# Seven maxima blocks of 128 query rows, and a rearranged end of the attention part, in a cross-attention and mixture-of-experts kernel

## The chip, the cores and the metric

The kernel runs on one core of a Trainium2 chip. The metric is the device time of one execution in microseconds (us). Engines are named as in the profile: PE (TensorE, matrix products; PEld is its loading of stationary operands), DVE (VectorE), ACT (ScalarE), POOL (GpSimd), and SP (SyncE), which here only issues transfers.

## The reference

The input x is 16 sequences of 224 rows of 512 numbers, and each has a context of 750 rows of 384. All is float32.

```
x = x + cross_attention(layernorm(x), ctx)       # 16 heads of 32, each with its softmax over 750 keys, then Wo
y = layernorm(x)
logits = cos(y, centroids) + y @ w_route.T       # 8 experts
gates  = softmax over the two largest logits, 0 elsewhere
x = x + sum over e of gates[e] * (gelu(y @ w1[e] + b1[e]) @ w2[e] + b2[e])
```

Only the two chosen experts of a row have a gate that isn't 0, so 2 x 3584 pairs of row and expert are enough.

## The kernel before

**Attention.** The work is cut into 64 groups (a sequence has four groups of four heads each). A Python loop over g from -2 to 68 writes out the order on each engine by hand; `first`, `second`, `third` and `fourth` are its bodies for g % 4 = 0 to 3, one of each on every engine, and `after(g)` follows each. It is a software pipeline. In turn g, PE projects Q and K of group g+2, finds maxima for group g+1, makes the scores and the weighted values of group g, and the denominators of group g-1. Products of float32 operands are made as three products of a high and a low part (`split3`). The high part is rounded by ACT, the low part is what DVE or POOL subtracts.

**Maxima.** The softmax needs a number to subtract for each query. `score_for_max(g, u)` multiplies one block of queries (stationary) by all 750 keys (moving, in two products of 376 columns), high parts only, into PSUM tile X, and DVE's `maximum(g, u)` reduces X to one column of `mx`. There are XU = 8 blocks of 112 rows for the 4 x 224 queries of a group. X is one tile, so block u+1 waits for DVE's reduction of block u. `transpose_max` turns `mx`, ACT negates it into `mneg`, and `put_max` (SP) copies it into a row of the stacked queries `qst`, from which the scores get their subtraction.

**Softmax sums.** ACT's `exps(g, s)` makes the probabilities from scores, 12 pieces for a group. POOL's `add_step(g, 0..4)` adds the six tiles of 125 keys in five steps into `psum_p`, `denominators(g)` on PE sums over the partitions with a matrix of ones, DVE's `invert` and `normalise` divide the output by it, ACT's `o_hi` and DVE's `o_lo` split it for the output projection (`project_o`).

**Second layernorm.** Per sequence b: DVE's `residual` and `y_stats`, POOL's `y_rsqrt` (16 small steps, two roots; semaphore newton2), ACT's `y_apply`, PE's transposes, ACT's copies to y_T, PE's `logits`, DVE's `keep_logits`.

**Weights of the experts.** w1 and w2 come in 16 pieces of 128x1024 (0 to 7 are w1). SP loads them (`load_pieces`), ACT rounds the high part (`w_part` on ACT), DVE subtracts the low part (`w_part` on DVE), in the turns 62 to 66 and one piece at the end.

**Routing.** After the loop DVE picks the two experts of each row (semaphore route), PE counts with a triangular matrix of ones, DVE makes the place of each pair in a list sorted by expert (place), and a table of which row stands in which of the 63 tiles of 128 slots is made on PE by one-hot products: `find_columns`, then `find_rows` in four chunks per choice, two choices. `table_done` ends it.

**Experts.** POOL gathers 128 rows with an indirect DMA, PE transposes (`fold_x`), multiplies by w1 (`up`), ACT does gelu, PE transposes (`fold_h`) and multiplies by w2 (`down`), DVE adds b2, ACT multiplies by the gate, and POOL adds the rows to the output with an indirect DMA.

What sets the order is the written-out sequence on each engine: an engine does its instructions strictly one after the other, and waits for semaphores in between. Names touched: `score_for_max` and `maximum` (L1540, L1072), `transpose_max` (L1549), `y_rsqrt` (from L539), `add_step` (L488, L491), `constants` (from L586), `w_part` (L846 on ACT, L1149 on DVE), `after` on each engine, `denominators` (L1590), `find_columns` (L1340, L1344), `find_rows` (L1352), `project_o` (L320 to L322 into M), `up` (L1804 to L1808), `down` (L1825 to L1827).

## Time and profile before

| | us |
|---|---|
| median of 3 runs | 1652.7 (1652.04 to 1652.82) |
| the profiled execution | 1648.43 |
| its span, first to last instruction | 1646.6 |
| PE busy in the span | 1524.2 (93%) |
| POOL, DVE, ACT busy | 1080.2, 1030.6, 944.2 |
| mean granted clock of PE | 0.964 |

```profile
PE   4899999999999999999999999999999743899997
PEclk9999999999999999999999999999999765899999
```

Each digit is a slice of 41 us, in tenths. PE is busy nearly throughout, except in the slices from the 32nd on (1276 us), where attention has ended and the experts haven't begun. PEclk is the granted clock: 1.2 GHz at 0.5 and 2.4 GHz at 1. The profiled execution is one run, shorter than the median of the timed ones by 4.3 us.

### The profile page before, as it was taken

How to read it: one execution, taken by the hardware profiler on the slowest of the kernel's cores; microseconds unless marked ns; L12 is line 12 of the kernel's file. 1: busy time of each engine (PE TensorE's matmuls, PEld its weight loads, DVE VectorE, ACT ScalarE, POOL GpSimd, SP SyncE). 2: the span in 40 equal slices, each digit the busy share in tenths (PEclk: the TensorE clock that was granted, in tenths of full speed). 3: DMA queues.
4: the chain of work that ended last, by engine and by line, in shares of the span. 5: the costliest groups of instructions: out<-in, count | busy, mean ns of one | idle time of the engine just before them, and what ended most of it. 6: DMA issues, size and time to landing. Idle time of an engine off the chain costs nothing.

```text
span 1646.6 us, 33344 instructions
## 1 busy us (share of the span) xinstructions
PE 1524.2 (93%) x11534; PEld 1247.4 (76%) x11534; DVE 1030.6 (63%) x1475; ACT 944.2 (57%) x2055; POOL 1080.2 (66%) x931
## 2 busy tenths in 40 slices
PE   4899999999999999999999999999999743899997
PEld 4777777778787878787877877877777433798996
DVE  5556666666666676766666666666665568344443
ACT  4456666666666666666666666665665440455554
POOL 3366767676767677776676777777775740477675
PEclk9999999999999999999999999999999765899999
DMA  7556666666667676767666757676756733578785
GB/s 193 97 81 111 101 134 123 110 124 108 127 110 134 111 129 112 131 110 139 112 130 107 136 101 144 101 140 101 140 91 120 187 122 35 136 135 147 135 148 90
DMA packets 113394, 199.29 MB, mean 121 GB/s; under 512 B 20448, under 2 KB 49280, under 8 KB 113104
## 3 DMA queue, kind: packets, MB, share of 16 engines
q1 hardware_dynamic: 98992, 165.81, 54.4%
q0 software_dynamic: 14240, 31.35, 10.5%
q8 instruction: 98, 1.61, 0.5%
q14 instruction: 64, 0.52, 0.1%
HBM read 64.29 MB, written 38.66 MB: 63 GB/s over the span
## 4 chain that ended last, share of the span: by engine, by line
PE 86%; DVE 5%; ACT 3%; POOL 2%; issue 1%; DMA 1%; POOLq 0%; DVEq 0%; SPq 0%; ACTq 0%
PE M L320 12%; PE S L1563 12%; PE M L321 12%; PE M L322 12%; PE X L1540 11%; PE O L1579 10%; ACT pr L781 2%; PE M L1825 2%; PE X L1807 2%; PE X L1808 2%; PE X L1806 2%; PE M L1826 2%; PE M L1827 2%; PE M L1590 2%; PE S L1796 2%
## 5 line engine op out<-in xcount | busy, mean ns | idle before, releaser
L1072 DVE TENSOR_REDUCE mx<-X 112x1 f32<-112x752 f32 x512 | 480.6, 939 | 356.0 <-PE X L1540 353.9
L491 POOL TENSOR_TENSOR psum_p<-psum_p,pr 125x896 f32<-125x896 f32 x256 | 543.9, 2124 | 172.6 <-ACT pr L781 149.1
L781 ACT ACTIVATE pr<-S 125x448 f32<-125x448 f32 x768 | 395.0, 544 | 224.4 <-PE S L1563 216.6
L1563 PEld LDWEIGHTS S<-qst,kst 128*125 128x125 f32 x1536 | 234.7, 189 | 113.0 <-ACT pr L781 51.2
L1563 PE MATMUL S<-qst,kst 128*125 128x224 f32 x1536 | 287.3, 291 | 27.1 <-ACT pr L781 21.2
L1540 PE MATMUL X<-kh_s,q_own 128*112 128x376 f32 x1024 | 272.0, 347 | 8.4 <-DVE mx L1072 7.9
L1540 PEld LDWEIGHTS X<-kh_s,q_own 128*112 128x112 f32 x1024 | 153.9, 176 | 48.0 <-issue 26.8
L1579 PE MATMUL O<-pr,v 125*32 125x224 f32 x3072 | 188.6, 364 | 1.7 <-ACT pr L781 1.7
L488 POOL TENSOR_TENSOR psum_p<-pr 125x896 f32<-125x896 f32 x64 | 135.6, 2119 | 80.1 <-ACT pr L781 79.9
L475 POOL TENSOR_TENSOR ctx_l<-ctx_r,ctx_h 128x750 fp32r<-128x750 f32 x48 | 85.4, 1811 | 74.7 <-ACT ctx_h L696 74.7
L320 PE MATMUL M<-ctx_h,wk_h 128*128 128x376 f32 (+1 forms) x384 | 130.0, 339 | 0.0
L321 PE MATMUL M<-ctx_l,wk_h 128*128 128x376 f32 (+1 forms) x384 | 129.4, 337 | 0.0
L322 PE MATMUL M<-ctx_h,wk_l 128*128 128x376 f32 (+1 forms) x384 | 128.8, 335 | 0.0
L1579 PEld LDWEIGHTS O<-pr,v 125*32 125x32 f32 x3072 | 81.3, 110 | 62.3 <-issue 23.1
L662 POOL DMA_INDIRECT out<-y_out,table_t x63 | 99.9, 1586 | 41.4 <-ACT y_out L1003 23.3
L654 POOL DMA_INDIRECT xg<-rows_d,table_x x63 | 62.4, 990 | 86.3 <-DVE settled L1400 43.0
L320 PE MATMUL M<-wv_h,ctx_h 128*125 128x512 f32 x288 | 116.8, 405 | 0.0
L322 PE MATMUL M<-wv_h,ctx_l 128*125 128x512 f32 x288 | 113.6, 394 | 0.0
L321 PE MATMUL M<-wv_l,ctx_h 128*125 128x512 f32 x288 | 113.5, 394 | 0.0
L1079 DVE RECIPROCAL M<-M 128x224 f32<-128x224 f32 x64 | 99.8, 1559 | 21.7 <-PE M L1590 21.6
L738 ACT ACTIVATE q_own<-qh_s,own 128x224 fp32r<-128x224 f32 x256 | 102.6, 472 | 2.1
L1062 DVE SCALAR_TENSOR_TENSOR kl_s<-M,bk_s,kh_s 128x376 fp32r<-128x376 f32 (+1 forms) x128 | 77.0, 602 | 14.3 <-ACT kh_s L749 14.1
(222 smaller groups left out, 3005.1 us busy)
## 6 DMA issues: line engine op xcount, KB each, us to landing
kst<-kh_s SPq DMA_DIRECT2D x128, 375.0 KB, 7.3
kst<-kl_s SPq DMA_DIRECT2D x64, 375.0 KB, 10.4
ctx_r<-ctxT SPq DMA_DIRECT2D x48, 375.0 KB, 12.2
qst<-qh_s SPq DMA_DIRECT2D x128, 112.0 KB, 2.8
rows_d<-x_res SPq DMA_DIRECT2D x32, 448.0 KB, 10.6
w_l<-w SPq DMA_DIRECT2D x16, 512.0 KB, 7.0
x_ln<-x SPq DMA_DIRECT2D x17, 448.0 KB, 11.0
qst<-ql_s SPq DMA_DIRECT2D x64, 112.0 KB, 3.0
```

Of the source, the lines that this page charges most:

```text
L320: pe.matmul(out, lhs[0], rhs[0], start=first, stop=False)
L321: pe.matmul(out, lhs[0], rhs[1], start=False, stop=False)
L322: return pe.matmul(out, lhs[1], rhs[0], start=False, stop=last)
L488: pool.tensor_tensor(out=total, in0=tiles[0], in1=tiles[1], op=ALU.add).then_inc(sum_step, 1)
L491: pool.tensor_tensor(out=total, in0=total, in1=tiles[half], op=ALU.add).then_inc(sum_step, 1)
L662: pool.indirect_dma_start(out=out[:, :], out_offset=bass.IndirectOffsetOnAxis(ap=table_t[:, i:i + 1], axis=0), in_=y_out[:, i % YO, :], in ...
L738: act.activation(q_own[:, g % 2, j, :], qh_s[:, g % 2, :], ACT.Copy, scale=own[:, j:j + 1]).then_inc(own_done, 1)
L781: act.activation(pr[0:KP, (3 * g + p) % 2, j, :, :], S[0:KP, n % SB, 0:2 * NQ].rearrange("p (i n) -> p i n", i=2), ACT.Exp).then_inc(exp_d ...
L1072: dve.tensor_reduce(mx[0:QP, u:u + 1], X[0:QP, :, 0:HALF[0][1]], AX.XY, ALU.max).then_inc(max_done, 1)
L1540: last = pe.matmul(X[0:QP, i, 0:w], q_own[:, g % 2, j, QP * qt:QP * (qt + 1)], kh_s[:, g % 2, off:off + w], start=True, stop=True)
L1563: last = pe.matmul(S[0:KP, n % SB, NQ * h:NQ * (h + 1)], kst[:, i, j, o:o + KP], qst[:, i, j, :], start=True, stop=True)
L1579: last = pe.matmul(O[HD * j:HD * (j + 1), 0:NQ], v[0:KP, 2 * p + i, HD * j:HD * (j + 1)], pr[0:KP, (3 * g + p) % 2, j, i, :], start=(p == ...
```

## The change

- Maxima: XU is 7. A block is 128 consecutive queries out of the group's 896, head by head, so a block can hold queries of two heads. Everything that had 112 rows here has 128. `maximum(g + 1, 7)` and `score_for_max(g + 1, 7)` are gone from all four bodies.
- Last roots: for the last two sequences (b = 14 and 15, LATE = 14) `y_rsqrt` is left out on POOL, and DVE does `late_root(b)` at the end of `y_stats(b)`, with 27 steps of Newton's method. `roots` and `shifted` count the semaphore.
- Sums: for the last group POOL leaves out steps 3 and 4, and `denominators` adds the last two tiles on PE, as two more sets of four products.
- Weight parts: ACT does 11 of them after turn 64 and 5 after turn 67; DVE 6 after turn 64, 4 after 66 and 6 behind `table_done`. PE waits for w1's before `up(0)` and for all before the first `down`. The first three loads on SP stand behind `put_max(63)`.
- `constants` on POOL moves from turn 63 to after turn 64. b2 (2 MB in SBUF) is loaded at the end of SP's loop, once the last output projection is done, instead of behind `table_done`; memory is laid out again for that, and `hot_row` becomes a ring of three chunks.
- `keep_clock(n)` on PE issues n products of 128x128 by 512 columns into a PSUM bank that nobody reads: 6 after turn 64, 22 after turn 65, 22 after the loop, 42 behind the counts, 10 ahead of each of the two choices' one-hot products, and 26 ahead of the first tile.

```diff
-XU = 8
+XU = GH * NQ // P
+LN_STEPS, Y_STEPS, LATE_STEPS = 8, 16, 2 * RSQRT_STEPS + 3
+LATE = B - 2
+ACT_EARLY = E + 3
+ROWS = 3 * CHUNK
...
+        def roots(b):
+            return Y_STEPS * min(b, LATE) + LATE_STEPS * max(0, b - LATE)
...
@@ on SP
-                    if g == GROUPS - 2:
-                        wait_full(sp, "K1", GROUPS - 1)
-                        load_pieces(0, 3)
...
-                        load_pieces(3, E)
+                        load_pieces(0, E)
+                wait_full(sp, "O1", B - 1)
+                sp.dma_start(b2_all[:, :, :], b2.rearrange("(a e) n -> a e n", a=1).broadcast_to([P, E, D])
+                             ).then_inc(b2_in, 16)
                 sp.wait_ge(route, 15)
...
-                sp.wait_ge(table_done, 1)
-                sp.dma_start(b2_all[:, :, :], b2.rearrange("(a e) n -> a e n", a=1).broadcast_to([P, E, D])
-                             ).then_inc(b2_in, 16)
...
@@ on POOL
-                    if not 0 <= g < GROUPS:
+                    if not 0 <= g < GROUPS or (g == GROUPS - 1 and i >= 3):
...
@@ on ACT
-                    if g == GROUPS - 2:
-                        for n in range(3):
-                            w_part(n)
...
-                        for n in range(3, E):
-                            w_part(n)
...
+                        wait_full(act, "den", GROUPS - 1)
+                        act.wait_ge(b1_both, 32)
+                        for n in range(ACT_EARLY):
+                            w_part(n)
+                    if g == GROUPS + NG - 1:
+                        for n in range(ACT_EARLY, W_PIECES):
                             w_part(n)
...
@@ on DVE
-                    dve.tensor_reduce(mx[0:QP, u:u + 1], X[0:QP, :, 0:HALF[0][1]], AX.XY, ALU.max).then_inc(max_done, 1)
+                    dve.tensor_reduce(mx[:, u:u + 1], X[:, :, 0:HALF[0][1]], AX.XY, ALU.max).then_inc(max_done, 1)
+                def late_root(b):
+                    n, m = roots(b), mv2[0:QP, :, :]
+                    v, y, tmp, off = ve2[0:QP, :], rstd2[0:QP, :], rtmp2[0:QP, :], shift2[0:QP, :]
+                    sq, ln = square[0:QP, :], length[0:QP, :]
+                    dve.wait_ge(y_var, QT * (b + 1))
+                    dve.wait_ge(yn_done, QT * b)
+                    rsqrt(dve, newton2, n, m[:, :, 1], EPS, ALU.add, v, y, tmp)
+                    n += RSQRT_STEPS
+                    dve.scalar_tensor_tensor(out=off, in0=m[:, :, 0], scalar=-1.0, in1=y, op0=ALU.mult,
+                                             op1=ALU.mult).then_inc(newton2, 1)
+                    wait_free(dve, "lg1", b - 1)
+                    dve.tensor_tensor(out=sq, in0=m[:, :, 1], in1=y, op=ALU.mult).then_inc(newton2, 1)
...
+                    rsqrt(dve, newton2, n + 3, sq, NORM_EPS2, ALU.max, v, ln, tmp)
...
+                    if b >= LATE:
+                        late_root(b)
...
                     if g == GROUPS:
-                        for n in range(E, E + 3):
+                        for n in range(6):
                             w_part(n)
...
-                        dve.wait_ge(newton2, Y_STEPS * B)
-                        for n in range(E + 3, 2 * E - 1):
+                        for n in range(6, 10):
                             w_part(n)
...
-                w_part(2 * E - 1)
...
                 dve.tensor_copy(settled[:, :], ones[:, 0:1]).then_inc(table_done, 1)
+                for n in range(10, W_PIECES):
+                    w_part(n)
...
@@ on PE
-                        last = pe.matmul(X[0:QP, i, 0:w], q_own[:, g % 2, j, QP * qt:QP * (qt + 1)],
+                        last = pe.matmul(X[:, i, 0:w], own_q[:, P * u:P * (u + 1)],
                                          kh_s[:, g % 2, off:off + w], start=True, stop=True)
...
+                    parts = [psum_p[0:KP, g % 2, :, :]]
+                    if g == GROUPS - 1:
+                        pe.wait_ge(sum_step, 5 * g + 3)
+                        pe.wait_ge(exp_done, 12 * (g + 1))
+                        parts += [pr[0:KP, (3 * g + 2) % 2, :, h, :] for h in range(2)]
...
+                def keep_clock(n, ready=w1_h[:, 0, 0:2, :].rearrange("p c n -> p (c n)")):
+                    for _ in range(n):
+                        pe.matmul(HP[:, 1, :], ready[:, 0:P], ready, start=True, stop=True)
+
                 def after(g):
+                    if g == GROUPS:
+                        keep_clock(6, wo_h[:, 0, :])
+                    if g == GROUPS + 1:
+                        pe.wait_ge(ew_hi, 1)
+                        keep_clock(22)
...
-                    score_for_max(g + 1, 7)
...
+                keep_clock(22)
                 pe.wait_ge(masks, 1)
                 pe.wait_ge(route, 12)
...
+                keep_clock(42)
                 for i in range(2):
+                    keep_clock(10)
                     pe.wait_ge(col_done, 2 * (i + 1))
...
+                keep_clock(26)
                 pe.wait_ge(which_done, 1)
                 pe.wait_ge(table_done, 1)
                 pe.wait_ge(b1_both, 32)
-                pe.wait_ge(ew_lo, W_PIECES)
                 fold_x(0)
                 fold_x(1)
+                pe.wait_ge(ew_lo, E)
                 e = expert_of(0)
                 up(0, e)
                 fold_h(0)
+                pe.wait_ge(ew_lo, W_PIECES)
```

## Rows read from the trace of the kernel before

**Rows 1.** Busy us by engine in three stretches, PE's granted clock, DMA share, GB/s.

```profile
97.40:1285.00 1187.60, 1166.23 (x9226) 937.39 (x9225) 784.27 (x1095) 734.05 (x1651) 837.33 (x712) 1.00 0.66 118
87.20:90.60 3.40, 3.40 (x23) 1.99 (x22) 1.16 (x2) 2.80 (x5) 2.39 (x2) 0.53 0.00 0
1346.70:1411.50 64.80, 26.98 (x120) 25.00 (x121) 44.24 (x75) 6.36 (x11) 11.07 (x22) 0.50 0.34 73
```

**Rows 2.** Groups by line, 400 to 1200: busy us, mean ns, idle before.

```profile
L320 PEld LDWEIGHTS M<-ctx_h,wk_h 128*128 128x128 f32 x240 | 45.3, 189 | 0.0
```

**Rows 3.** Timeline of PE, turns 37 and 39: start, us, instructions, idle before.

```profile
804.34 0.50 PE L1540 MATMUL X<-kh_s,q_own 128*112 128x376 f32 x2
804.68 0.39 PE L320 MATMUL M<-wo_h,oT_h 128*112 128x512 f32 x1
...
844.82 0.48 PE L1563 MATMUL S<-qst,kst 128*125 128x224 f32 x2 [0.83 <-ACT pr L781]
```

**Rows 4.** Timeline of PE in turn -1.

```profile
48.74 0.60 PE L1540 MATMUL X<-kh_s,q_own 128*112 128x376 f32 x2 [1.03 <-DVE mx L1072]
50.47 0.34 PE L1549 MATMUL M<-id_s,mx 112*8 112x112 f32 x1 [1.12 <-DVE mx L1072]
```

**Rows 5.** Timelines of DVE and POOL: a step at the start, two instructions at 837.

```profile
19.22 0.15 DVE L45 TENSOR_TENSOR ctmp<-cinv 8x1 f32<-8x1 f32 x1
...
837.41 2.13 POOL L488 TENSOR_TENSOR psum_p<-pr 125x896 f32<-125x896 f32 x1
...
837.47 2.32 DVE L1093 SCALAR_TENSOR_TENSOR oT_l<-o_s,bv_s,oT_h 128x224 fp32r<-128x224 f32 x1
```

**Rows 6.** Timeline of POOL before turn 63.

```profile
1297.07 10.41 POOL L491 TENSOR_TENSOR psum_p<-psum_p,pr 125x896 f32<-125x896 f32 x4 [3.97 <-ACT pr L781]
```

**Rows 7.** Timeline of DVE between attention and experts.

```profile
1308.65 1.57 DVE L1079 RECIPROCAL M<-M 128x224 f32<-128x224 f32 x1
...
1321.51 10.33 DVE L1149 TENSOR_TENSOR w_l<-w_l,w_h 128x1024 fp32r<-128x1024 f32 x5 [0.67 <-ACT w_h L846]
1331.76 1.55 DVE L1079 RECIPROCAL M<-M 128x224 f32<-128x224 f32 x1
...
1350.45 4.63 DVE L1149 TENSOR_TENSOR w_l<-w_l,w_h 128x1024 fp32r<-128x1024 f32 x4 [5.17 <-POOL length L570]
...
1355.88 0.42 DVE L1259 TENSOR_REDUCE most<-lgs 112x32 f32<-112x256 f32 x1
...
1394.87 0.15 DVE L1400 COPY settled<-ones 128x1 f32<-128x1 f32 x1
```

**Rows 8.** Timeline of ACT in the same stretch.

```profile
1318.06 2.31 ACT L781 ACTIVATE pr<-S 125x448 f32<-125x448 f32 x4
...
1334.16 4.83 ACT L846 ACTIVATE w_h<-w_l 128x1024 fp32r<-128x1024 f32 x5
1347.82 1.52 ACT L812 ACTIVATE x_res<-x_ln,shift,rstd 112x512 f32<-112x512 f32 x2 [8.82 <-POOL shift L552]
```

**Rows 9.** Timeline of PE in the same stretch, and the first tile.

```profile
1328.63 0.98 PE L1590 MATMUL M<-psum_p,ones 125*32 125x224 f32 x8 [6.48 <-POOL psum_p L491]
...
1385.48 7.01 PE L1786 MATMUL M<-hot_tok,hot_row 112*128 112x64 f32 x32 [2.06 <-DVE hot_row L1352]
...
1406.04 0.58 PE L1804 MATMUL X<-b_hl,ones_r 128*128 x1 [0.78 <-DVE xTs L1404]
...
1412.69 0.40 PE L1825 MATMUL M<-w_h,hTs 128*128 x1
```

**Rows 10.** The chain that ended last, in order of time: start, us, what.

```profile
1334.88 0.74 PE M L320
...
1336.05 0.43 PE M L322
...
1339.84 0.23 PE M L322
```

**Rows 11.** The gathers into xg: time to landing.

```profile
DMA to landing us min/median/max: 3.3/4.3/7.3
```

More of the change, by code:

```diff
@@ L171, in expert_phase @@
         rw = sb("rw", [P, DC, 2 * E])
-        mneg = sb("mneg", [XU, QP], F32R)
-        zone_end = here[0]
+        mneg = sb("mneg", [XU, P], F32R)
+        here[0] = zone_end = max(here[0], zone_c + 4 * (E * D + ROWS * P + TT * LC))
         bq_s, bk_s, bv_s = sb("bq_s", [P, NG]), sb("bk_s", [P, NG]), sb("bv_s", [P, NG])
@@ L316, in residual_of, with shifted @@
             return x_ln if b == B - 1 else x_res
+        def roots(b):
+            return Y_STEPS * min(b, LATE) + LATE_STEPS * max(0, b - LATE)
+        def shifted(b):
+            return roots(b) + (LN_STEPS if b < LATE else RSQRT_STEPS + 1)
         def split3(pe, out, lhs, rhs, first, last):
@@ L531, in y_rsqrt @@
                 def y_rsqrt(b):
-                    if not 0 <= b < B:
+                    if not 0 <= b < LATE:
                         return
@@ L599, in after @@
                         return
+                    constants()
                     pool.wait_ge(pv_done, 3 * GROUPS)
@@ L639, in fourth @@
                     y_rsqrt(b - 1)
-                    constants(g)
                     add_step(g, 0)
@@ L1151, in after @@
                 def after(g):
-                    if g == GROUPS - 2:
-                        for n in range(3):
-                            w_part(n)
                     if g == GROUPS - 1:
@@ L1158, in after @@
                                           op=ALU.subtract).then_inc(b1_lo, 1)
-                        for n in range(3, E):
-                            w_part(n)
                     if g == GROUPS:
-                        for n in range(E, E + 3):
+                        for n in range(6):
                             w_part(n)
@@ L1548, in transpose_max @@
                     pe.wait_ge(max_done, XU * (g + 1))
-                    pe.transpose(out[0:XU, 0:QP], mx[0:QP, :], id_s[0:QP, 0:QP]).then_inc(full, 1)
+                    pe.transpose(out[0:XU, 0:P], mx[:, :], id_s[:, :]).then_inc(full, 1)
                 def score(g, s):
@@ L1587, in denominators @@
                     out, full = claim("den", g)
-                    pe.wait_ge(sum_step, 5 * (g + 1))
-                    for j in range(GH):
-                        last = pe.matmul(out[HD * j:HD * (j + 1), 0:NQ], ones[0:KP, :], psum_p[0:KP, g % 2, j, :],
-                                         start=True, stop=True)
+                    parts = [psum_p[0:KP, g % 2, :, :]]
[3 more added lines that the diff above has]
+                        parts += [pr[0:KP, (3 * g + 2) % 2, :, h, :] for h in range(2)]
+                    else:
+                        pe.wait_ge(sum_step, 5 * (g + 1))
+                    for n, part in enumerate(parts):
+                        for j in range(GH):
+                            last = pe.matmul(out[HD * j:HD * (j + 1), 0:NQ], ones[0:KP, :], part[:, j, :],
+                                             start=n == 0, stop=n == len(parts) - 1)
                     last.then_inc(full, 1)
@@ L1694, in second @@
                     score(g, 9)
-                    score_for_max(g + 1, 7)
                     project_o(b - 1, 1, 1)
@@ L1728, in third @@
                     score(g, 9)
-                    score_for_max(g + 1, 7)
                     values(g, 1)
@@ L1765, in fourth @@
                     transpose_y(b - 1, 1)
-                    score_for_max(g + 1, 7)
                     score(g, 10)
```

76 lines of the change are left out of this document (39 added, 37 removed).

## The prediction

> **What bounds the kernel now.** I read the windows first, then the groups by line of the steady middle, then the timelines of PE and of the engines that PE waits for. From 97 to 1285 us PE is busy 1166 of 1188 us, at full granted clock; DVE (784), ACT (734) and POOL (837) have a third of that time free [rows 1]. There a microsecond that leaves PE's queue leaves the run, unless something else ends last at that place. From 1285 to 1411 us it is another kernel: a chain in which DVE, POOL, ACT and PE wait for each other, with PE busy 27 of its last 65 us and at half clock [rows 1]. There PE's instructions are cheap and everything on the chain counts. From 1412 us the 63 expert tiles fill PE again; the change leaves them alone.
>
> **Maxima: seven blocks for eight.** Per head group score_for_max issues two products of 376 moving columns per block, over 64 groups: 1024 products become 896. The queries become the stationary operand's columns, 128 instead of 112. A load of 128 columns takes 189 ns where K does it [rows 2], beside the products, since PEld overlaps PE; the K products, with the same 376 moving columns, follow each other no slower than the maxima's. So I price a new pair like an old one: from the start of the eighth block to the start of what follows is 804.68 - 804.34 = 0.34 us [rows 3]. (If a product's cost went with the stationary columns, 7x128 = 8x112, the gain would be 0; that is the other end.) DVE loses one tensor_reduce in eight, off the path.
> Where the block only fills a wait, it gains nothing. In every fourth group it stands between the y transposes and score 10; score 10 waits 0.83 us for the exponentials behind it, which ACT does after copying y_T out of PSUM [rows 3]. Those copies start from the transposes, which stand before the block, so the wait grows by 0.34 and the group gains 0. That is 14 of the groups up to 61. In the other three kinds output projection, logits or values follow, all longer than an exponential.
> At the start the block costs more, since PE waits for DVE between blocks: 50.47 - 48.74 = 1.7 us in group -1 [rows 4]; with about 0.7 and 1.4 in groups 0 and 1, where the same two waits are shorter, 3.7 us. Groups 2 to 61: 46 x 0.34 = 15.8. **Main part: -19.5 us.**
>
> **Last roots on DVE.** The 27 tiny instructions of late_root are queued on DVE before invert(62). Alone, such a step takes 0.15 us [rows 5] and some 0.04 to the next (0.19, 5.1 us in all, the same as POOL's chain of 5.2). But they don't run alone: at 837.47 a DVE instruction with two SBUF inputs, usually 0.44 us, took 2.32, until POOL's addition that began at 837.41 had ended [rows 5]. 21 of the 27 have two SBUF inputs. late_root(14) would start at 1299.9, and POOL adds four times from 1297.07 on [rows 6], now 2.13 us each since no weight parts slow it, to 1305.7. So DVE gets through its three first steps and about one per addition; at 1305.8, 21 are left. Ten fit in until add_step(63, 0), from 1307.8 to 1309.9, blocks it again; the rest is done at 1311.9. invert(62), at 1308.65 before [rows 7], then starts 3.2 us later, and with it o_hi(62), the exponentials 4 to 7 of the last group that ACT has behind it, the values, y_apply and the transposes. Exponentials 8 to 11, which ran from 1318.06 to 1320.4 [rows 8], end at 1323.6. Bounds: 0 (free slots between additions; -2.7, since additions end earlier) and +6.
> The Trainium skill, page SBUF — State Buffer (the single rule on ports), says the same: a DVE instruction with two SBUF inputs waits for a GpSimd instruction that reads SBUF, for its whole length. It also says that DVE's one-input instructions can contend in a two-port mode; that would add the six tensor_scalar steps, at most 1 us more here.
>
> **Sums partly on PE, and weight parts later.** Three of ACT's weight parts stood ahead of the last group's first exponential. Without them (3 x 0.97 us at most [rows 8]) scores 0 to 2 go earlier, but score 3 stands behind den(62), which waits for POOL's additions to 1305.8: worth nothing. SP issues the loads of these three behind the maxima's transfer instead of ahead of it; POOL makes its constants after group 64's work, idle since 1320.9, in time for the b1 transfers. Before, invert(63) started at 1331.76 because DVE sat in five weight parts, 10.33 us at 2.07 each beside POOL's four additions [rows 7]. After: the exponentials end at 1323.6. den's four products took 0.98 us at half clock [rows 9], so the last eight of the values take 1.7 and den's twelve now 2.9 (PE sums the last two tiles itself, so nothing waits for POOL): 1328.3. invert, normalise, o_hi and o_lo take 3 us: 1331.3. PE has been dense since 1323.7 (values, den, logits 14, six dummies) and should be at full clock by now, so logits and dummies end about there, and output projection starts at 1332 instead of 1334.88 and takes 24 x 0.23 = 5.6 [rows 10]: 1337.6.
> Now DVE is late: after(64) puts six weight parts ahead of the residual. They cost 1.15 each without POOL (4.63 / 4 [rows 7]): 1332.0 + 6.9 = 1338.9; ACT's halves take 0.97 [rows 8] and keep ahead. Statistics start at 1340.2, 3.3 earlier than before. late_root(15) meets an idle POOL: 13 steps to the shift, 2.5 us, against 2.8 on POOL; y_apply at 1344.4, before 1347.82 [rows 8]. The 22 dummies behind the projection (5.1 us at full clock) end at 1342.7, before the transposes at 1346. DVE: late_root ends 1347.0, mask, four weight parts, 1351.9; logits 15 are ready by 1350. The routing (DVE most) starts at 1352.8, before 1355.88 [rows 7]: **-3.1**. This is a small part of what the moved work seems to free.
> Routing to table: the same DVE chain of 39 us, less the weight part in it (1.15) and about 0.35 for the two count products, of 512 columns each, at full clock: **-1.5**. The ring of three row chunks stalls nothing: PE takes 1.75 us for a chunk at half clock (7.01 / 4 [rows 9]), DVE makes one in 1.14 and has 4.6 us of columns between the halves.
> Table to first product: up(0) started 11.0 us after the table (1395.02) [rows 7, 9]. Its first fold waited for a gather that landed in 7.3 us, the longest of all, beside the 2 MB load of b2; the median is 4.3 [rows 11]. With b2 moved forward (issued about 1344 behind the stores of x and x_n; the gates' small transfers queue behind its 2 MB, but aren't needed before 1391) the first lands at about +5.2. But six weight parts now stand before x_low(0): 6.9 + 0.7 + 0.1 = 7.7: **-3.3**. Bounds: -5 (no weight parts in the way) and +2 (each also waits about 1 us for a gather's POOL instruction). I take the undisturbed one, as the four parts beside POOL's DMA issue at 1350.45 took 1.16. The page named above would side with it: descriptors need the write side, these parts only the shared read side.
>
> **Dummies.** 138 products of 512 columns: 32 us at full clock (0.23 each), 59 at half (0.43) [rows 10]. What they give: from up(0) to down(0) took 1412.69 - 1406.04 = 6.65 us at half clock [rows 9]; at full 13 x 0.12 for up, then gelu, fold, up again: 4.25. Idle ahead of the first fold is about 3.4 us, so I expect the clock to hold mostly: **-2.1**. Where the cover goes: 52 stand between the count products and the first row chunk, 14.2 us apart; at full clock they take 12.1, if the first 16 run at half 15.2, which delays PE but not DVE; all at half 22.4, 8 too many. The 26 before the gather have 8.7 us.
>
> **Sum.** -19.5 - 3.1 - 1.5 - 3.3 - 2.1 = -29.5 us. The profiled execution took 1648.4 (span 1646.6), so 1618.9 by it; the runs' median is 1652.7, 4.3 above, and 29.5 off that is **1623.2**. Half of the tail's possible gain is handed back by late_root(14) and by weight parts ahead of the residual.
>
> **Rivals.**
> A, late_root isn't blocked as I price it, and slots between additions are enough: the tail gains 3 to 6 more, 1618. For it: additions are separate instructions with gaps; against it: the one row where a DVE instruction paid the whole addition. 0.2.
> B, dummies in the way: the clock stays at half for most of the tail, as for the 65 us before 1411.5 [rows 1]. They then overrun by about 1 (behind projection), 3 (behind logits), 8 (52) and 3 (26), and the 2.1 and 0.35 don't come: +15 with what the ring adds, 1638. Against it: the projection alone, 24 products, was enough for full clock. 0.12.
> C, the block isn't worth 0.34 us: the stream behind it is bound by ACT's exponentials and not by PE in other groups too (third kind: scores 7 to 9 already go at ACT's pace). With half the gain, +9: 1632. Against it: PE idles only 22 us in 1188. 0.12.
> D, the other side of zero: the clock in the main part. A wait of ACT of 2.3 us ahead of 87.2 was followed by a stretch of 3.4 us at half clock, and again at 94 [rows 1], worth 1.7 us each of full work. The wait in each fourth group grows from 0.83 to 1.2. If that drops the clock for two stretches each time, 14 x 3.4 = 48 us is lost against 29.5 won: 1671. It decides from nine such double stretches on. Against it: none of the waits of 0.8 did it. 0.03.
> The changes that don't do what they say at all (products priced by stationary columns) would leave 1643: 0.03.
>
> **How the numbers follow.** My case has 0.5, with its own range 1619 to 1628; A 0.2, B 0.12, C 0.12, D 0.03, the last 0.03. From 1613 (A with its far end) to 1636 (C, and most of B) holds eight in ten. Slower by over 0.2%, which is what a measurement of this kernel can tell from no change: only D, 0.03, and some of B and C together: 0.04. Within 0.2%: 0.02. Faster: 0.94.
>
> **What would show it.** The step between max transposes of the steady groups: three of four shorter by 0.34 us, the fourth unchanged, with its wait at about 1.2. DVE's steps in late_root(14): some of 2 us, invert(62) later than add (62, 4) by 6 us. den(63) right behind the values; DVE's weight parts ahead of the residual. The first gather landing in 4 to 5 us, DVE in weight parts as x_low(0) becomes ready. Full clock from the projection to the tiles. The forecast is wrong if PE's idle time in the main part grows by more than 10 us, or if dummies end later than what stands behind them was ready.

## The result

| | before | changed |
|---|---|---|
| median of the timed runs | 1652.37 (4 runs, 1651.11 to 1652.82) | 1635.62 (4 runs, 1632.63 to 1635.79) |
| the profiled execution, its span | 1648.43, 1646.6 | 1635.56, 1633.7 |
| mean granted clock of PE | 0.964 | 0.984 |

The ratio is 0.9897, 95% interval 0.9881 to 0.9912: 16.7 us faster, where 29.5 were forecast. The time lies in the range (1613 to 1636), at its slow end, 12.4 us above the predicted 1623.2. The changed kernel was measured once more in a later session, after_again below: there it is 22.6 us faster than before, so 7 to 13 us of the forecast gain are missing.

Where the 12.9 us between the two profiled executions come from. The end of turn 60, the last quiet place before the tail, is taken from the third-last max transpose; the rows behind it count from there.

| | before | changed | difference | forecast |
|---|---|---|---|---|
| end of turn 5 | 172.42 | 165.68 | -6.7 | |
| end of turn 60 | 1261.30 | 1253.49 | -7.8 | -19.5 |
| to the table's end | 133.3 | 129.2 | -4.1 | -4.6 |
| table to the third tile's h low part | 24.0 | 18.9 | -5.1 | -5.4 |
| from there to the end of the span | 227.9 | 232.1 | +4.1 | 0 |

So nearly the whole miss lies in the main part: 11.7 us, and 0.8 in the two rows of the tail. The last row is probably no part of it. The first three gains add up to 17.0 us, which is what the medians show (16.7), while the profiled execution of before is 3.9 us shorter than its own median; the last section has what is known of that.

The chain that ended last, as shares of the span, from the pages; first before, then changed:

```profile
PE 86%; DVE 5%; ACT 3%; POOL 2%; issue 1%; DMA 1%; POOLq 0%; DVEq 0%; SPq 0%; ACTq 0%
```

```profile
PE 62%; POOL 18%; issue 9%; DVE 6%; ACT 4%; DMA 1%; POOLq 0%; DVEq 0%; SPq 0%; ACTq 0%
POOL psum_p L509 12%; PE M L342 8%; PE S L1581 8%; PE M L343 8%; PE M L344 8%; PE X L1558 7%; PE O L1597 6%; POOL ctx_l L493 3%; ACT pr L797 2%; PE X L1840 2%; PE X L1842 2%; PE X L1841 2%; POOL x_res L525 2%; PE M L1615 2%; PE M L1859 2%
```

The engine that was said to have a third of its time free now carries a fifth of the chain. The time between max transposes tells in which bodies (mean of 13 or 14 turns each, 6 to 60; the runs' names are those of the experiments):

| us per turn | before | changed | maxima_only | bo_later | both | ctx_split | guard |
|---|---|---|---|---|---|---|---|
| `first` | 19.92 | 19.63 | 19.62 | 19.62 | 19.62 | 19.63 | 19.63 |
| `second` | 20.69 | 20.90 | 20.67 | 20.44 | 26.30 | 21.42 | 20.42 |
| `third` | 18.68 | 18.70 | 18.70 | 18.70 | 18.44 | 18.43 | 18.44 |
| `fourth` | 19.96 | 19.97 | 19.96 | 19.96 | 19.96 | 19.97 | 19.97 |

`first` pays back 0.29, `fourth` nothing, as forecast. `second` and `third` were to give 0.34 each, gave nothing, and `second` grew by 0.21. Over the turns 6 to 60 that is 7 us short in `second` and 5 in `third`. Groups by line from 400 to 1200 us (count, busy us, mean ns, idle before and what ended it), POOL's addition of bo and PE's denominators; before, then changed:

```profile
L507 POOL TENSOR_TENSOR x_res<-x_res,bo_s 112x512 f32<-112x512 f32 x20 | 25.4, 1291 | 18.8 <-DMA x_res<-x 18.8
L1590 PE MATMUL M<-psum_p,ones 125*32 125x224 f32 x324 | 23.6, 362 | 0.0
```

```profile
L525 POOL TENSOR_TENSOR x_res<-x_res,bo_s 112x512 f32<-112x512 f32 x20 | 25.2, 1283 | 33.8 <-DMA x_res<-x 33.8
L1615 PE MATMUL M<-psum_p,ones 125*32 125x224 f32 x320 | 23.4, 363 | 6.4 <-POOL psum_p L509 6.3
```

And one `second` (turn 41, in which POOL waited longest) and the `third` behind it in the changed kernel's timelines of POOL and PE (start, us):

```profile
860.80 2.53 POOL L525 TENSOR_TENSOR x_res<-x_res,bo_s 112x512 f32<-112x512 f32 x2 [4.27 <-DMA x_res<-x]
863.28 4.36 POOL L509 TENSOR_TENSOR psum_p<-psum_p,pr 125x896 f32<-125x896 f32 x2
...
867.79 0.59 PE L1615 MATMUL M<-psum_p,ones 125*32 125x224 f32 x8 [1.27 <-POOL psum_p L509]
...
873.92 5.33 POOL L493 TENSOR_TENSOR ctx_l<-ctx_r,ctx_h 128x750 fp32r<-128x750 f32 x3 [4.21 <-ACT ctx_h L712]
879.22 8.89 POOL L509 TENSOR_TENSOR psum_p<-psum_p,pr 125x896 f32<-125x896 f32 x4
...
888.25 0.59 PE L1615 MATMUL M<-psum_p,ones 125*32 125x224 f32 x8 [0.20 <-POOL psum_p L509]
```

In `second`, POOL stood 4.27 us in `add_bo`, for a load, and the two additions behind it ended 1.27 us too late for den. In `third`, den waited for a chain that begins with ACT's ctx_high behind exponential 7: 5.33 of ctx_low, then four additions, end to end.

How near the two chains were to den before the change can be read from the traces (medians over 13 or 14 turns each; the load's times count from the start of `second`, the last two rows give the time from the end of POOL's last addition to the start of den):

| us | before | maxima_only | changed | bo_later | guard |
|---|---|---|---|---|---|
| `second`: x_res load issued | -1.88 | -0.59 | -0.58 | -0.53 | -1.21 |
| `second`: load landed | 1.91 | 3.25 | 3.54 | 3.34 | 2.32 |
| `second`: last addition to den | 1.32 | 0.15 | 0.15 | 4.87 | 4.85 |
| `third`: last addition to den | 0.15 | 0.15 | 0.15 | 0.15 | 1.88 |

Where den waits for the addition, 0.15 us pass between the two. `third` shows that same 0.15 before the change: there was next to no slack. `second` had some 1.2 us in the median turn, more than the 0.34 of a block, and lost it another way: SP issues the load when the stores of x_n have landed, these took 11.8 us instead of 11.0 in a turn that had become shorter, and the load landed 1.6 us later in the turn.

### The profile page after: what moved, and what is told of

Its sections match the earlier page's. It is cut to its first block, busy times and chain, and to the rows that moved or that the text cites. A ratio compares the mean times of both kernels' runs of the same rounds, so it can differ in the third digit from the quotient of the medians.

```text
span 1633.7 us, 33542 instructions
## 1 busy us (share of the span) xinstructions
PE 1534.6 (94%) x11560; PEld 1251.7 (77%) x11560; DVE 961.4 (59%) x1465; ACT 943.3 (58%) x2055; POOL 1066.8 (65%) x897
## 4 chain that ended last, share of the span: by engine, by line
PE 62%; POOL 18%; issue 9%; DVE 6%; ACT 4%; DMA 1%; POOLq 0%; DVEq 0%; SPq 0%; ACTq 0%
POOL psum_p L509 12%; PE M L342 8%; PE S L1581 8%; PE M L343 8%; PE M L344 8%; PE X L1558 7%; PE O L1597 6%; POOL ctx_l L493 3%; ACT pr L797 2%; PE X L1840 2%; PE X L1842 2%; PE X L1841 2%; POOL x_res L525 2%; PE M L1615 2%; PE M L1859 2%
## 5 line engine op out<-in xcount | busy, mean ns | idle before, releaser
L509 POOL TENSOR_TENSOR psum_p<-psum_p,pr 125x896 f32<-125x896 f32 x254 | 536.2, 2111 | 177.9 <-ACT pr L797 154.6
L1079 DVE TENSOR_REDUCE mx<-X 128x1 f32<-128x752 f32 x448 | 421.4, 941 | 366.8 <-PE X L1558 364.6
L1558 PE MATMUL X<-kh_s,q_own 128*128 128x376 f32 x896 | 241.4, 351 | 5.9 <-DVE mx L1079 5.9
L1558 PEld LDWEIGHTS X<-kh_s,q_own 128*128 128x128 f32 x896 | 145.7, 190 | 43.9 <-issue 35.7
```

The costliest lines, as they stand in the source:

```text
L509: pool.tensor_tensor(out=total, in0=total, in1=tiles[half], op=ALU.add).then_inc(sum_step, 1)
L1079: dve.tensor_reduce(mx[:, u:u + 1], X[:, :, 0:HALF[0][1]], AX.XY, ALU.max).then_inc(max_done, 1)
L1558: last = pe.matmul(X[:, i, 0:w], own_q[:, P * u:P * (u + 1)], kh_s[:, g % 2, off:off + w], start=True, stop=True)
```

## Experiments

Theory T: a removed block saves PE what was priced, but in `second` a load's wait on POOL (x_res, add_bo, additions, den) and in `third` ctx_high, ctx_low, additions, den end last and take it back. Rivals: R1, a product costs with its stationary columns; R2, the loss comes from something in the rest of the change. All ratios are to the kernel before on the same chip; runs 1 to 4, 5 to 8 and 9 to 12 shared a chip each.

| run | median us | ratio, 95% |
|---|---|---|
| maxima_only | 1636.9 | 0.9945 (0.9930 to 0.9960) |
| rest_only | 1635.2 | 0.9933 (0.9919 to 0.9946) |
| bo_later | 1623.0 | 0.9850 (0.9835 to 0.9864) |
| both | 1701.2 | 1.0330 (1.0313 to 1.0347) |
| ctx_split | 1635.1 | 0.9919 (0.9904 to 0.9934) |
| root14_pool | 1619.2 | 0.9830 (0.9808 to 0.9851) |
| w_split | 1624.8 | 0.9866 (0.9848 to 0.9884) |
| no_dummies | 1627.7 | 0.9882 (0.9865 to 0.9900) |
| after_again | 1629.4 | 0.9862 (0.9846 to 0.9877) |
| guard | 1619.6 | 0.9822 (0.9803 to 0.9842) |
| best | 1619.1 | 0.9802 (0.9788 to 0.9815) |
| few_dummies | 1617.7 | 0.9791 (0.9778 to 0.9804) |

**maxima_only and rest_only**: the change in two halves.

```diff
 # maxima_only: the kernel before, and
-XU = 8
+XU = 7        # with mneg, mx, maximum, score_for_max, transpose_max as in the change
 # rest_only: the changed kernel, with these back at 8 blocks of 112
```

> The kernel before with nothing but the seven maxima blocks; roots, sums, weight parts and dummies as before. My forecast gave this part 19.5 us (3.7 at the start, 46 groups x 0.34). Theory T: PE does save 0.34 per block, but POOL's chains give most of it back: x_res landing later behind the fixed issue of the store of x_n, then POOL's additions, then den in every second kind of group; and ctx_high, ctx_low, additions, den in every third kind. Then the gain is 6 to 8 us, the second kind of group is not shorter than before (20.7 to 20.9 us), and PE's den waits for psum_p by name in many groups. Rival R1 (a product costs with its stationary columns, 7x128 = 8x112): no group is shorter and the gain is the 4 to 5 us of the start. Rival R2 (the main part's loss comes from something in the rest of the change): 17 to 20 us faster than before.

> The changed kernel with eight maxima blocks of 112 queries again; late roots, sums on PE, moved weight parts and dummies stay. My forecast gave these parts 3.1 + 1.5 + 3.3 + 2.1 = 10.0 us. If they act only behind group 61: 9 to 10 us faster than before, and with the maxima alone at 6 to 8 the two gains add up to the whole of 16.7. If the two parts disturb each other (R2), the sum of the two single gains is 5 us or more above 16.7.

Measured by the ratios: -9.1 and -11.0 us, each about 1 more than expected (by the medians -10.5 and -12.2). `second` of maxima_only is 20.67 us, den waited 3.9 us for psum_p, and `first` is 0.30 shorter: T stands; R1 falls, since `first` would not be shorter; R2 falls as the main cause, since the maxima alone fall 7.5 us short of their 19.5 by the end of turn 60 (1249.29). It isn't excluded for the rest: in the changed kernel `second` is another 0.2 us longer and turn 60 ends 4.2 us later than in maxima_only. In no_dummies, whose code up to there is the changed kernel's, turn 60 ends at 1249.89, so part of it is a matter of the execution or the chip. The two gains add up to 20.1 us by the ratios (22.7 by the medians) against 16.7 and 22.6 in the two sessions of the changed kernel: no disturbance between the halves that these intervals can tell.

**bo_later**: the wait for x_res behind the additions' need.

```diff
                 def first(g, b):            # POOL
                     ...
-                    if b < B:
-                        add_bo(b - 1)
                 def second(g, b):
                     add_step(g - 1, 3)
                     add_step(g - 1, 4)
                     add_step(g, 0)
+                    if b < B:
+                        add_bo(b - 1)
                     ctx_low(b + 1)
```

> The changed kernel; POOL's add_bo, which waits for the load of x_res, moves from the end of the first kind of group to behind the first addition of the second kind, so that the additions behind it no longer wait for that load. T: the wait of POOL for x_res goes (about 3 us of it per group of 4), PE's den in the second kind no longer waits, and this kind goes from 20.9 to about 20.35 us; the third kind stays as it is (18.70): 14 groups x 0.5 = 7 us faster than the changed kernel, about 1628.5. R1 or any cause on PE itself: same as the changed kernel within 1 us. If add_bo in the new place makes other additions late instead, 0 to 3 us slower.

`second` fell from 20.90 to 20.44 (expected 20.35), the end of turn 60 came 7.25 us earlier (5.3 against after_again's), and the ratio fell by 0.0047 against the first session (0.0012 against after_again, which the intervals hardly separate; the turns do). POOL no longer waits for the load, den a third as long as before:

```profile
L525 POOL TENSOR_TENSOR x_res<-x_res,bo_s 112x512 f32<-112x512 f32 x20 | 25.5, 1300 | 0.0
L1615 PE MATMUL M<-psum_p,ones 125*32 125x224 f32 x328 | 23.8, 361 | 2.3 <-POOL psum_p L509 2.3
```

**both**: and ctx_high ahead of o_hi, for `third`.

```diff
                 def second(g, b):           # ACT, on top of bo_later
                     xT_part(b + 1, 1)
+                    ctx_high(b + 1)
                     o_hi(g - 1)
                     ...
                     exps(g, 7)
-                    ctx_high(b + 1)
```

> add_bo moved as in the run before, and ACT's ctx_high of the second kind of group moved ahead of its exponentials 5 to 7, so that POOL's ctx_low and the additions behind it start earlier. T: besides the 7 us of the second kind, the third kind of group gets its 0.34 us: 18.70 to about 18.4, 14 x 0.3 = 4 us; in all 10 to 12 us faster than the changed kernel, about 1624.5. If the third kind is held by something else (PE itself, ACT's exponentials), the run is like the one before, or slower by what ctx_high (0.8 us on ACT) delays the exponentials behind it: up to 14 x 0.8 = 11 us.

`third` came out as T says, 18.44. But `second` took 26.30, and the run was 78 us slower than bo_later; I had expected a miss of at most 11, by the exponentials. The timelines of DVE, POOL and PE show it (start, us):

```profile
832.31 5.46 DVE L1100 SCALAR_TENSOR_TENSOR oT_l<-o_s,bv_s,oT_h 128x224 fp32r<-128x224 f32 x1
```

```profile
832.25 5.27 POOL L493 TENSOR_TENSOR ctx_l<-ctx_r,ctx_h 128x750 fp32r<-128x750 f32 x3
...
838.76 0.96 PE L1558 MATMUL X<-kh_s,q_own 128*128 128x376 f32 x2 [3.72 <-DVE mx L1079]
```

DVE's oT_l subtraction of 0.44 us, with two SBUF inputs, began 0.06 us after POOL's and ended only behind three of POOL's, back to back. DVE's next maxima were late, PE stood 3.72 us, and the granted clock was 0.50 for the next 5 us. One collision cost 5.9 us a turn.

**ctx_split**: the same aim, one ctx_high part each behind exponentials 5, 6 and 7.

```diff
                     exps(g, 5)
+                    ctx_high(b + 1, 0)
                     exps(g, 6)
+                    ctx_high(b + 1, 1)
                     exps(g, 7)
-                    ctx_high(b + 1)
+                    ctx_high(b + 1, 2)
```

> add_bo later as in the run bo_later; besides, ACT's three parts of ctx_high in the second kind of group stand one each behind exponentials 5, 6 and 7 instead of all behind 7. The run before, which had all three ahead of exponential 4, made the third kind of group 18.44 us, as T wants, and lost 5.9 us in the second kind, where DVE's oT_l subtraction took 5.46 us beside POOL's three ctx_l subtractions. If that collision is the whole of the loss: here oT_l is through before the first ctx_l, the second kind stays at 20.4 to 20.5, the third goes from 18.70 to 18.45 to 18.6, and the run is 1.5 to 3.5 us faster than bo_later's (0.985 of before), about 0.983. If instead ACT's delayed exponentials were the loss: the second kind grows by 0.3 to 0.8 us, 4 to 11 us slower than bo_later.

oT_l was out of the way and `third` 18.43, but `second` grew by 0.98, for what the second theory named: PE waited for exponentials that stood behind a ctx_high part (0.84 us each). PE's timeline in one turn:

```profile
877.51 0.48 PE L1582 MATMUL S<-qst,kst 128*125 128x224 f32 x2 [0.32 <-ACT pr L796]
878.66 0.96 PE L1598 MATMUL O<-pr,v 125*32 125x224 f32 x16 [0.68 <-ACT pr L796]
```

These 1.00 us are the loss. By the ratios the run is some 11 us slower than bo_later.

**guard**: ctx_high early as in both, at a place where ACT is idle for 2.68 us in ctx_split, waiting for o_s (0.53 us are left of that in guard), and POOL held back by one wait.

```diff
                 def second(g, b):           # POOL, on top of both
                     if b < B:
                         add_bo(b - 1)
+                    if b + 1 < B:
+                        pool.wait_ge(ol_done, g)
                     ctx_low(b + 1)
```

> The kernel of the run both (add_bo later, ctx_high ahead of o_hi, 78 us slower than bo_later), with one wait more: POOL starts its three ctx_low subtractions only when DVE's oT_l subtraction of the same group is through. If the collision of these two is the whole loss: oT_l takes 0.44 us again, the second kind of group goes from 26.3 to 20.3 to 20.5 us, the third stays at 18.44 since ctx_low still ends 2 us earlier than in bo_later and no exponential is held up, and the run is 3 to 5 us faster than bo_later's (0.985): about 0.982 of before. If DVE's maxima or ACT's order were the loss in both: still over 1.0.

POOL waited 0.61 us, oT_l took 0.44, and den no longer waits for POOL at all:

```profile
863.02 0.44 DVE L1102 SCALAR_TENSOR_TENSOR oT_l<-o_s,bv_s,oT_h 128x224 fp32r<-128x224 f32 x1
...
863.54 5.31 POOL L493 TENSOR_TENSOR ctx_l<-ctx_r,ctx_h 128x750 fp32r<-128x750 f32 x3 [0.61 <-DVE oT_l L1102]
...
L1617 PE MATMUL M<-psum_p,ones 125*32 125x224 f32 x328 | 23.8, 362 | 0.0
```

`second` 20.42 and `third` 18.44: the ratio is 0.051 below that of both, some 84 us, for one wait. The end of turn 60 lies at 1241.33, 20.0 us ahead of before, where 19.5 had been forecast for the maxima. The sum agrees partly by luck: 10.9 us of it were won in the turns 6 to 60, where 13.9 had been forecast (41 x 0.34), and 9.1 before them, where some 5 had been. Whether the two moves on POOL would give something to the kernel with eight blocks wasn't tried; its den did not wait.

**root14_pool and best**: the roots of batch 14 back on POOL.

```diff
-LATE = B - 2
+LATE = B - 1      # root14_pool on bo_later; best on guard
```

> add_bo later as in bo_later; besides, LATE is B-1: the roots of batch 14 are POOL's again, only those of batch 15 stay on DVE. My forecast priced late_root(14) on DVE at +3.2 us, since its steps wait for POOL's additions of 2.1 us. If that holds: invert(62) starts within 11 us of the last max transpose as before, the last exponentials end at 21.4 us behind it instead of 25.1, and the run is 3 to 4 us faster than bo_later's. Rival: the den of group 62 waits for POOL, which has 5.2 us of roots ahead of its additions, and gives half of it back: 1 to 2 us. Rival A of my forecast (no blocking): same or slower.

> The kernel of guard, and the roots of batch 14 on POOL again (LATE is B-1). The runs so far: add_bo later -7.5 us against the changed kernel, roots of 14 back on POOL -3.5, guard -3.7. If they add up: 14 to 15 us faster than the changed kernel, ratio to before about 0.980. If the ends of groups 61 and 62 differ between kernels by POOL's order alone, up to 2 us less.

The steps of the tail, counted from the end of turn 60, in one execution each:

| us | before | changed | after_again | rest_only | bo_later | root14_pool | guard | best | no_dummies |
|---|---|---|---|---|---|---|---|---|---|
| invert(62) | 47.4 | 51.3 | 53.4 | 49.2 | 50.5 | 47.6 | 49.8 | 47.7 | 50.5 |
| last exponential ends | 59.1 | 63.5 | 65.6 | 60.9 | 62.4 | 59.2 | 60.8 | 59.4 | 61.6 |
| invert(63) | 70.5 | 67.4 | 69.5 | 64.6 | 66.1 | 61.5 | 63.0 | 61.6 | 63.9 |
| routing starts | 94.6 | 91.5 | 93.6 | 88.7 | 90.2 | 86.7 | 87.1 | 86.6 | 87.9 |
| table done | 133.3 | 129.2 | 131.4 | 126.3 | 127.9 | 124.4 | 125.0 | 124.5 | 125.7 |
| first x_low | 143.9 | 136.4 | 138.5 | 133.5 | 135.0 | 131.5 | 132.1 | 131.6 | 132.8 |
| third h_low | 157.4 | 148.1 | 150.3 | 145.2 | 146.7 | 143.4 | 143.9 | 143.4 | 146.3 |

The changed kernel and after_again are the same code and differ by 2 us in every row, so differences of 1 or 2 us between columns aren't resolved. With the roots on POOL the exponentials end 3.2 us earlier than in bo_later and the table comes 3.5 us earlier: expected 3 to 4. Counted from the last max transpose the exponentials end 6.2 us earlier (18.7 against 24.8), but POOL's roots make turns 61 and 62 3.0 us longer (40.6 against 37.6). In best against guard it is 1.4 and 0.5: there DVE's weight parts, which set the residual, now wait for ACT's high halves (0.85 us). By the times the step isn't resolved: 0.9830 against 0.9850, and 0.9802 against 0.9822, each with intervals that touch.

**w_split**: three of the six weight parts behind the table moved behind x_low(1).

```diff
-                for n in range(10, W_PIECES):
-                    w_part(n)
...
                 dve.wait_ge(which_done, 1)
+                for n in range(10, 13):
+                    w_part(n)
                 x_low(0)
                 e = expert_of(0)
                 x_low(1)
+                for n in range(13, W_PIECES):
+                    w_part(n)
```

> add_bo later as in bo_later; besides, of DVE's six weight parts behind the table three stand ahead of x_low(0) as before and three behind x_low(1). In the changed kernel the table stood 7.69 us ahead of up(0), with DVE in weight parts until x_low(0) was ready. If these set the time: up(0) comes 5.5 to 6 us behind the table, the down product then waits for the last part (3.5 us behind x_low(1)) no longer than for h, and 1.5 to 2 us are won against bo_later. If POOL's gathers, whose issue took 1.9 us each beside these parts, set it: with three parts fewer beside them they take about 1 us again and the gain is the same or up to 1 us more. If the landing of the gather sets it: less than 0.5 us.

No gain. The first x_low came 7.06 us behind the table, in bo_later 7.14: neither theory's 1.5. PE's timeline:

```profile
1377.69 1.07 PE L1653 MATMUL X<-w_h 128*128 128x512 f32 x4
1378.60 0.60 PE L1831 MATMUL S<-id_s,xg 128*128 128x128 f32 x4
...
1385.44 0.92 PE L1831 MATMUL S<-id_s,xg 128*128 128x128 f32 x4 [1.76 <-DVE w_l L1176]
```

The last of the 26 dummies ends where the fold begins, 5.7 us behind the table (the gather had landed 0.8 us before); without dummies the fold began at 5.0 and then took 1.09 us at half clock instead of 0.60. The fold and ACT's rounding of 0.60 us follow before x_low can start, so in bo_later weight parts, dummies and the gather all end last within less than a microsecond. And the expectation that the down product would wait no longer was wrong: the third fold waits 1.76 us for the moved parts, from up(0) to down(0) it takes 8.2 us (4.8 in bo_later), and the third h_low comes 3.5 us later behind the table.

**no_dummies and few_dummies**: without all 138, and without the first 50.

```diff
-                    for _ in range(n):        # no_dummies, on the changed kernel
+                    for _ in range(0):
 # few_dummies, on best: the keep_clock calls 6, 22 and 22 ahead of the counts are gone
```

> The changed kernel as it is (add_bo in its old place), with none of the products that nobody reads. My forecast gave them 2.1 us at up to down of the first tile, and 0.35 for the count products, and let the projection and den get to full clock without them. If that is right: 2 to 5 us slower than the changed kernel (ratio to before 0.991 to 0.993). If they do nothing (the clock falls and rises where real work is): same. If they stood in the way (those behind the logits end as the routing's sums are ready, den and others waited half a us): 1 to 2 us faster.

> The kernel of best without the 50 products that nobody reads in front of the routing (6, 22 and 22); the 88 behind it stay. Without all of them the first tile's up to down took 1.4 us longer, at half clock, and nothing ahead of the table was later, although the last output projection ran at half clock: DVE's weight parts end after it anyway. So the 50 are worth nothing: same as best within 1 us. If they hold the clock for what follows the routing's start: up to 1 us slower. If they stand in the way of the count products: 0.5 us faster.

> The changed kernel once more, on the chip of the runs below, so that they can be held against it. Its two profiled executions are also to tell how far the expert tiles vary: from the third h_low to the end its first profile shows 232.1 us, seven other kernels with the same tiles 226.9 to 228.2. If that is a matter of the execution: 226.9 to 228.2 here, and a ratio of 0.989 to 0.991. If it belongs to the kernel: 232 again.

after_again is a miss on both counts. The ratio is 0.9862, below the expected 0.989 to 0.991, and its interval doesn't meet the first session's; the time from the third h_low to the end is 232.1 us again. So a repetition of the same code moved by 6 us of median (1635.62 and 1629.38, with before at 1652 both times), and what moved it wasn't found.

From the first x_low to the third h_low: 13.5 us without dummies (as before, 13.5), 11.8 in the changed kernel, 12.4 in few_dummies: the dummies save 1.8 us there, forecast 2.1. Up to the table they bring nothing: routing to table takes 37.8 us with and without. The last output projection does start at half clock without them (some nine products, PE's timeline of no_dummies), but DVE's weight parts end only together with it (both at 1324.2):

```profile
1316.87 0.46 PE L342 MATMUL M<-wo_h,oT_h 128*112 128x512 f32 x1 [1.52 <-DVE oT_l L1100]
...
1317.96 0.63 PE L342 MATMUL M<-wo_h,oT_h 128*112 128x512 f32 x1
```

As a whole no_dummies is no slower than the changed kernel (0.9882 against 0.9897 and 0.9862): 1.8 us is below what the times tell. few_dummies is the fastest kernel measured, 0.9791, 11.6 us less than the changed one on the same chip; against best it is the same within the intervals.

## Why the prediction came out as it did

- **Maxima, "46 x 0.34 = 15.8": the step that failed.** The price of a block was near (0.25 to 0.30 in the turns where nothing else ends last). What failed was the condition: "the other three kinds" was argued from PE's next instruction and ACT's exponentials alone, and POOL was dismissed with "a third of that time free" [rows 1]. That is a mean over unlike turns. In `third` before, den already started 0.15 us behind POOL's last addition, as it does where it waits for it: next to no slack, and this, not 30% idle, was the number to look for. In `second` the slack of 1.2 us (0.3 in the tightest turn) was larger than a block in most turns; there the prediction left out that POOL's additions stand behind a load whose time follows the stores and not PE's turns. That wait of 18.8 us in 800 stood in the trace before, and grew to 33.8. Rival C named the size (half the gain lost) but the wrong engine, ACT.
- **The start, 3.7 us**: 4.6 by the end of turn 1. Right in kind (its three terms, 1.7, 0.7 and 1.4, add up to 3.8). The fourth kind with no gain: right, and its wait for the exponentials grew from 0.83 to 1.18 us, as forecast (1.2).
- **late_root(14), +3.2 us**: right. Exponentials 8 to 11 end at 25.1 us behind the last max transpose, 21.4 before: +3.7 (24.7 to 25.2 in after_again, rest_only, bo_later and ctx_split). DVE's timeline in the changed kernel, beside POOL's additions:

```profile
1291.76 0.64 DVE L41 TENSOR_SCALAR ve<-mv 112x2 f32<-112x2 f32 x1
1292.43 0.17 DVE L42 TENSOR_SCALAR rstd<-ve 112x2 int32<-112x2 int32 x1
1292.64 1.99 DVE L43 TENSOR_SCALAR rstd<-rstd 112x2 int32<-112x2 int32 x1
1294.66 0.16 DVE L45 TENSOR_TENSOR rtmp<-rstd 112x2 f32<-112x2 f32 x1
1294.85 2.00 DVE L46 SCALAR_TENSOR_TENSOR rtmp<-rtmp,ve 112x2 f32<-112x2 f32 x1
...
1297.08 1.98 DVE L45 TENSOR_TENSOR rtmp<-rstd 112x2 f32<-112x2 f32 x1
...
1301.54 2.06 DVE L47 SCALAR_TENSOR_TENSOR length<-rtmp,length 112x2 f32<-112x2 f32 x1
...
1304.81 1.57 DVE L1086 RECIPROCAL M<-M 128x224 f32<-128x224 f32 x1
```

```profile
1290.27 8.78 POOL L509 TENSOR_TENSOR psum_p<-psum_p,pr 125x896 f32<-125x896 f32 x4 [5.46 <-ACT pr L797]
1301.51 2.07 POOL L506 TENSOR_TENSOR psum_p<-pr 125x896 f32<-125x896 f32 x1 [2.47 <-ACT pr L797]
```

  One step is lost per addition. Two of the blocked ones (L43, 1.99 us, and in part L41) are tensor_scalar with one SBUF input: what the Trainium skill (SBUF — State Buffer, Who interferes with whom) says, that a tensor_scalar in a two-port mode also waits for GpSimd's whole instruction, fits this; the trace shows that it waited, not the mode.
- **Sums and weight parts, -3.1 to the routing**: measured -3.1 (94.6 to 91.5), but -1.0 in after_again, so that the number agrees so well is luck. The path was the forecast one: projection started 70.5 (before 73.6), DVE's six parts ended behind it and set the residual:

```profile
1324.44 6.89 DVE L1176 TENSOR_TENSOR w_l<-w_l,w_h 128x1024 fp32r<-128x1024 f32 x6
1331.24 1.28 DVE L1109 TENSOR_TENSOR x_ln<-M,x_ln 112x512 f32<-112x512 f32 x2
...
1344.94 0.42 DVE L1276 TENSOR_REDUCE most<-lgs 112x32 f32<-112x256 f32 x1
```

- **Routing to table, -1.5**: 38.7 to 37.8, -0.95. The weight part's 1.15 went; the 0.35 for the counts did not come (in no_dummies this stretch is as long).
- **Table to up(0), -3.3**: 11.0 to 7.7, right, with DVE in weight parts until x_low(0) was ready. The bound beside it, weight parts that wait for gathers, did not come: they took 1.15 us each. It was the other way round: POOL's gather instructions took 1.9 us beside DVE's weight parts, and 0.95 behind them:

```profile
1383.06 6.89 DVE L1176 TENSOR_TENSOR w_l<-w_l,w_h 128x1024 fp32r<-128x1024 f32 x6
1389.87 0.68 DVE L1423 TENSOR_TENSOR xTs<-S,xTs 128x512 fp32r<-128x512 f32 x1
```

```profile
1384.01 1.20 POOL L670 DMA_INDIRECT xg<-rows_d,table_x  x1 [58.44 <-DVE settled L1417]
1385.52 1.86 POOL L670 DMA_INDIRECT xg<-rows_d,table_x  x1 [0.30 <-issue]
1387.68 1.95 POOL L670 DMA_INDIRECT xg<-rows_d,table_x  x1 [0.31 <-issue]
1389.93 0.94 POOL L670 DMA_INDIRECT xg<-rows_d,table_x  x1 [0.30 <-issue]
```

  The forecast followed a row with plain DMA issues (1.16 us for four parts); for the indirect ones that row was no guide, and what I had read out of the Trainium skill (SBUF — State Buffer, Who interferes with whom), that DVE's subtractions leave the gathers alone, is not borne out for the second and third of them. In w_split, with three parts fewer there, the third took 0.94.
- **Dummies, -2.1**: 1.8, and the clock held where it was forecast. Full clock to the tiles did not hold all the way: from 1338 to 1348 the granted clock was 0.51, through the last transposes and logits. None of rival B's overruns of 8 us came.
- **Rivals.** A (no blocking) is refuted by the four steps of 2 us; B by no_dummies; D by the main part's granted clock of 1.00; the stationary-column price by `first`.

## What to carry to other kernels

Before a cut on the bounding engine is priced, go through each repeated body and take, for every wait of that engine that doesn't show because it is met, how long before it the other side was ready; the smallest of these is the most that the cut may give, whatever the share of idle time is. It may give less where the other side is timed by a transfer that doesn't move with the shorter turn, like the load of x_res here. Move waits for loads behind the instructions that somebody is waiting for. When an instruction on POOL is moved, look at which DVE instructions with two SBUF inputs it will lie beside: one semaphore wait that kept them apart was worth some 84 us here.

## What the runs showed of the hardware

- A DVE instruction blocked by POOL isn't let in between POOL's instructions when these follow each other without a wait: oT_l was held for three of 1.8 us (5.46 us in both). Between additions that wait for each other's semaphore, one DVE instruction or a few got through each time.
- The same 63 expert tiles took two different times. From the third h_low to the end of the span: 226.8 to 228.3 us in the profiles of before, maxima_only, rest_only, bo_later, ctx_split, root14_pool, w_split and no_dummies; 231.2 to 232.2 in those of the changed kernel, after_again, guard, best and few_dummies. None of the edits touches the tiles, and the last four are all the runs of one chip. The kernel before also has a median of 1652.0 there, and 1647.4 and 1646.6 on the two chips of the other runs, so it goes with the chip or the hour rather than with the kernel, against what after_again's expectation would conclude. In the changed kernel's profile PE's waits without a cause (issue) ahead of `up`'s first product are 2.0 us, in before's 0.3, and those of its weight load 4.8 against 1.0. What sets them wasn't found. It bears on how near two kernels of different chips can be compared by their times. It doesn't explain why the changed kernel stood at 0.9897 once and at 0.9862 the other time, since before had 1652 in both sessions.
- PE's granted clock was different at one place of the tail between kernels whose instructions there are the same: values and den of group 63 took 1.7 and 2.1 to 2.4 us in the changed kernel, after_again, rest_only, bo_later and ctx_split, at half clock, and 0.97 and 1.3 in the other kernels with the sums on PE, at full. From the last exponential to invert(63) it is 3.7 to 3.9 us in the former and 2.2 to 2.3 in the latter, which alone moves everything behind by some 1.5 us. What decided it wasn't looked into.
